# Start-up order of an adaptive-norm router kernel: condition weights, experts and the first transposes

## What is computed

```python
W = weights[condition]                       # one [128, 128] matrix of 16 for each sample
flat = einsum('bct,bcd->bdt', x, W).reshape(B * 128, 2048)
logits = flat @ router_weight.T + router_bias
topk_w, topk_idx = top_k(softmax(logits), 8)
w_dense = zeros(B * 128, 64).at[rows, topk_idx].add(topk_w)
out = x + (flat * topk_w.sum(-1) + w_dense @ expert_bias).reshape(x.shape)
```

## Time and profile before

| | |
|---|---|
| three runs | 558.46, 559.57 and 559.75 us, median 559.57 |
| the profiled execution's own time | 558.69 us |
| its span in the profile | 556.9 us |
| TensorE matmuls busy | 541.0 us, 97% of the span |
| VectorE, ScalarE, GpSimd busy | 471.2, 368.5 and 354.4 us |
| mean granted TensorE clock | 0.993 |

### The profile page before, as it was taken

The page is one execution under the profiler, slowest core; times in us unless marked ns, Lnnn a source line. Parts: engine busy times, 40 slices in busy tenths (PEclk is TensorE's granted clock), DMA queues, the critical chain, the costliest instruction groups (busy, mean ns, idle before and its releaser), DMA issues.

```text
span 556.9 us, 12892 instructions
## 1 busy us (share of the span) xinstructions
PE 541.0 (97%) x3360; PEld 477.0 (86%) x3360; DVE 471.2 (85%) x1055; ACT 368.5 (66%) x836; POOL 354.4 (64%) x326
## 2 busy tenths in 40 slices
PE   5879999999999999999999999999999999999997
PEld 5768888888888888888888888888888888888875
DVE  2488898988889988889988889898888998888975
ACT  3576666677666677666677666667666667766661
POOL 0176666766666776666776666676666677666676
PEclk9979999999999999999999999999999999999999
DMA  8986999888999888898888999888899888889245
GB/s 243 311 201 231 309 297 279 292 300 287 297 318 276 269 311 289 295 325 280 292 276 296 294 311 300 271 290 297 286 298 315 284 283 295 288 294 326 119 166 212
DMA packets 70850, 155.96 MB, mean 280 GB/s; under 512 B 6322, under 2 KB 45234, under 8 KB 62770
## 3 DMA queue, kind: packets, MB, share of 16 engines
q1 hardware_dynamic: 70834, 155.77, 85.6%
HBM read 88.64 MB, written 67.11 MB: 280 GB/s over the span
## 4 chain that ended last, share of the span: by engine, by line
PE 93%; DMA 3%; SPq 1%; ACT 1%; issue 1%; DVE 1%; ACTq 0%; DVEq 0%
PE zt_ps L337 21%; PE xt_ps L325 14%; PE p_ps L390 11%; PE p_ps L387 11%; PE p_ps L385 11%; PE p_ps L386 10%; PE p_ps L391 10%; PE scores_ps L360 2%; DMA out_sb<-L_ffn_expert_bias 2%; PE scores_ps L369 1%; PE scores_ps L351 1%; DMA cond_sb<-itok_B 1%; SPq L243 0%; SPq L244 0%; DVE xt_lo L546 0%
## 5 line engine op out<-in xcount | busy, mean ns | idle before, releaser
L681 POOL TENSOR_TENSOR x_lo<-x_sb,x_hi 128x512 fp32r<-128x512 f32 x256 | 327.0, 1308 | 176.2 <-ACT x_hi L459 176.2
L546 DVE TENSOR_TENSOR xt_lo<-xt_ps,xt_hi 128x512 fp32r<-128x512 f32 x256 | 175.7, 687 | 63.6 <-ACT xt_hi L451 60.8
L451 ACT CAST xt_hi<-xt_ps 128x512 fp32r<-128x512 f32 x256 | 148.2, 582 | 102.9 <-PE xt_ps L325 84.9
L612 DVE SCALAR_TENSOR_TENSOR out_sb<-p_ps,w_sum,x_sb 128x512 f32<-128x512 f32 x256 | 189.6, 740 | 6.2 <-PE p_ps L391 6.2
L459 ACT CAST x_hi<-x_sb 128x1024 fp32r<-128x1024 f32 x128 | 133.7, 1045 | 0.5 <-PE p_ps L391 0.5
L337 PE MATMUL zt_ps<-xt_hi,router_hl 128*128 128x256 f32 x512 | 129.6, 285 | 4.5 <-DVE xt_lo L546 4.5
L337 PE MATMUL zt_ps<-xt_lo,router_hl 128*128 128x256 f32 x512 | 129.2, 285 | 0.0
L325 PE MATMUL xt_ps<-ident,x_sb 128*128 128x128 f32 x784 | 119.2, 277 | 0.1
L385 PE MATMUL p_ps<-x_hi,w_hl 128*128 128x512 f32 x256 | 118.8, 464 | 0.0
L337 PEld LDWEIGHTS zt_ps<-xt_hi,router_hl 128*128 128x128 f32 x512 | 98.1, 192 | 11.0 <-DVE xt_lo L546 5.2
L337 PEld LDWEIGHTS zt_ps<-xt_lo,router_hl 128*128 128x128 f32 x512 | 98.4, 192 | 4.8
(11 more groups left out here) (38 smaller groups left out, 368.7 us busy)
## 6 DMA issues: line engine op xcount, KB each, us to landing
out<-out_sb SPq DMA_DIRECT2D x126, 512.0 KB, 4.2
x_sb<-x SPq DMA_DIRECT2D x62, 1024.0 KB, 6.8
x_turn<-x SPq DMA_DIRECT2D x120, 128.0 KB, 4.7
w_sb<-L_cond_weights SPq DMA_DIRECT2D x64, 64.0 KB, 5.3
x_sb<-x SPq DMA_DIRECT2D x4, 256.0 KB, 6.0
x_sb<-x SPq DMA_DIRECT2D x2, 512.0 KB, 8.0
out_sb<-L_ffn_expert_bias SPq DMA_DIRECT2D x2, 512.0 KB, 9.4
out<-out_sb SPq DMA_DIRECT2D x4, 256.0 KB, 2.5
```

The costliest lines, as they stand in the source:

```text
L451: act.copy(xt_hi[:, n % 2, :, r, :], xt_ps[v % 4][:, :].rearrange("p (q c) -> p q c", c=P)).then_inc(xt_hi_ready, 1)
L546: dve.tensor_tensor(xt_lo[:, n % 2, :, r, :], xt_ps[v % 4][:, :].rearrange("p (q c) -> p q c", c=P), xt_hi[:, n % 2, :, r, :].bitcast(F32) ...
L612: dve.scalar_tensor_tensor(out_sb[:, r, cols], p_ps[n % 2][:, :], w_sum[:, o % 2, r:r + 1], x_sb[:, (2 * o + r) % XRING, cols], ALU.mult, ...
L681: pool.tensor_tensor(x_lo[:, r, cols], x_sb[:, (2 * o + r) % XRING, cols], x_hi[:, r, cols].bitcast(F32), ALU.subtract).then_inc(x_lo_read ...
```

## The change

SP: the conditions are loaded third, ahead of the router's second half. The x pair of unit 1 is issued ahead of the wait for the conditions and of all weights; the weights of units 0 and 1 follow. TensorE: slot 0 of unit 0 is transposed right after the router's first half, and its cast and subtraction stand between the two halves of the router's cast and subtraction; the first route waits for the first half only, the third for both. Experts: the cast and subtraction leave ScalarE and VectorE; GpSimd makes four copies and four subtractions of 512 columns each, in the step of unit 1, between `w_low` of unit 1 and `x_low` of unit 0.

```diff
             load_first(0, slice(0, PIECE), first_loaded)
+            sp.dma_start(cond_sb[:, :], condition).then_inc(cond_loaded, 16)
             sp.dma_start(router_sb[:, HALF:T], router_weight[:, HALF:T]).then_inc(router_loaded[1], 16)
             load_first(1, slice(0, PIECE), first_loaded)
-            sp.dma_start(cond_sb[:, :], condition).then_inc(cond_loaded, 16)
             for r in range(2):
                 load_first(r, slice(PIECE, HALF), second_loaded)
             for r in range(2):
                 load_first(r, slice(HALF, T), x_loaded)
-            sp.wait_ge(cond_loaded, 16)
-            for r in range(2):
-                load_weights(0, 0, r)
             for r in range(2):
                 load(0, 1, r)
-            for r in range(2):
-                load_weights(0, 1, r)
+            sp.wait_ge(cond_loaded, 16)
+            for o in range(2):
+                for r in range(2):
+                    load_weights(0, o, r)
...
-            sp.wait_ge(router_in_ps, 1)
+            sp.wait_ge(router_in_ps, 2)
...
-            last.then_inc(router_in_ps, 1)
+                if q == TB // 2 - 1:
+                    last.then_inc(router_in_ps, 1)
+                if t == TB // 2 - 1:
+                    transposes(0, 0, 0)
...
-                    elif new:
+                    elif new and (i, v) != (0, 0):
                         transposes(m, i, v)
...
                         if i == 2 and v == 0:
-                            pe.wait_ge(expert_ready, 1)
+                            pe.wait_ge(expert_ready, PIECES)
                         project(m, i - 2, v)
...
-                        if i == 0 and v == 3:
-                            pe.wait_ge(router_ready, 2)
+                        if i == 0 and v in (3, 7):
+                            pe.wait_ge(router_ready, 1 + v // 7)
                         route(m, i, v // 2 - 1)
...
-            act.wait_ge(router_in_ps, 1)
             for g in range(2):
+                act.wait_ge(router_in_ps, g + 1)
                 act.copy(router_hl[:, g * TB // 2:(g + 1) * TB // 2, 0, :],
                          p_ps[g][:, :].rearrange("p (t e) -> p t e", e=E)).then_inc(router_hi_ready, 1)
+                if g == 0:
+                    xt_high(0, 0, 0)
...
-                    if i == 1 and v == 4:
-                        act.wait_ge(expert_loaded, 32)
-                        act.copy(expert_hl[:, :], expert_sb).then_inc(expert_hi_ready, 1)
...
                                   ALU.subtract).then_inc(router_ready, 1)
+                if g == 0:
+                    xt_low(0, 0, 0)
...
-                    if i == 1 and v == 6:
-                        dve.wait_ge(expert_hi_ready, 1)
-                        dve.tensor_tensor(expert_hl[E:2 * E, :], expert_sb[E:2 * E, :],
-                                          expert_hl[E:2 * E, :].bitcast(F32),
-                                          ALU.subtract).then_inc(expert_ready, 1)
...
+            def split_experts():
+                pool.wait_ge(expert_loaded, 32)
+                for n in range(PIECES):
+                    cols = slice(n * PIECE, (n + 1) * PIECE)
+                    pool.tensor_copy(expert_hl[:, cols], expert_sb[:, cols]).then_inc(expert_hi_ready, 1)
+                pool.wait_ge(expert_hi_ready, PIECES)
+                for n in range(PIECES):
+                    cols = slice(n * PIECE, (n + 1) * PIECE)
+                    pool.tensor_tensor(expert_hl[E:2 * E, cols], expert_sb[E:2 * E, cols],
+                                       expert_hl[E:2 * E, cols].bitcast(F32),
+                                       ALU.subtract).then_inc(expert_ready, 1)
+                pool.wait_ge(expert_ready, PIECES)
...
                     for r in range(2):
                         w_low(m, i, r)
+                if i == 1:
+                    split_experts()
                 if mid:
                     x_low(m, i - 1, 0)
```

More of the change, by code:

```diff
@@ L517, in step @@
                             w_high(m, i, r)
-                    if i == 1 and v == 4:
-                        act.wait_ge(expert_loaded, 32)
-                        act.copy(expert_hl[:, :], expert_sb).then_inc(expert_hi_ready, 1)
                     if mid and v == 1:
                         zt_copy(m, i - 1)
-                    if new:
+                    if new and (i, v) != (0, 0):
                         xt_high(m, i, v)
@@ L646, in step @@
                         if i == 2 and v == 0:
-                            dve.wait_ge(expert_ready, 1)
+                            dve.wait_ge(expert_ready, PIECES)
                         finish(m, i - 2, v)
```

## The result

The changed kernel takes 564.83 us (median; 564.53 to 565.16), the kernel before 559.66 on the same chips: ratio 1.0092, interval 1.0070 to 1.0115, so 5.2 us slower. 563.7 was forecast, in a range of 560.0 to 567.5. The profiled execution took 564.53 us and has a span of 562.7 us against 556.9, 5.8 more.

A forecast was written before the change was run, and what follows sets the result against it. TensorE, busy throughout 100 to 500 us, bounds the kernel, so early delays carry through one for one. First projection at 41.4 against 36.4 gives +5.0 us on the profiled 558.69: 563.7 us, range 560.0 to 567.5.

The forecast's parts named there:

- SP's order: SP's load queue: first weights land at 19.1, 5.6 us later; TensorE idles 6.3 us, second route at 20.9.
- Rival 1: Weight queue, 7 to 19 us: first weights do not wait for the second x pair; 557.2 us; chance 0.14.
- Conditions third, first slot between the halves: SP's loads and the first unit's slot 0: these moves cost nothing and gain nothing.
- The clock, first fall: TensorE after the 6.3 idle us: half clock from 20.9 to 27.2, for 6.26 us.
- Rival 2: TensorE's second route: the clock does not fall in the 6.3 idle us; +2.2 us, 560.9; chance 0.09.
- GpSimd as the last wait: Before the first projection: GpSimd's expert split ends at 40.1, the x subtraction the projection needs at 41.4.
- That is late next: GpSimd's expert copies and subtractions, 8.4 us, end at 40.1; the needed x subtraction takes 1.3 more, to 41.4.
- rival 3: TensorE idle from about 36.1 to 38.2 and 40.2 to 41.4: clock falls once more; 2.7 us, 566.4; chance 0.14.
- TensorE ready at 40.2: After the route at 38.2, a route and eight transposes end at 40.2; TensorE could project from there.
- The forecast 41.4: End of GpSimd's x subtraction that the first projection needs, compared with the mark of 36.4: +5.0 us.

The follow-up runs named there:

- e1: The changed kernel with the first unit's weights issued ahead of the second x pair again; median 557.95 us, ratio 0.9983.
- e2: The kernel before with only the second x pair issued ahead of the wait for the conditions and of all weights; median 565.26 us, ratio 1.0100.
- e4: The kernel before with only conditions third and the first unit's slot 0 between the router's halves; median 558.12 us, ratio 0.9971.
- e5: The changed kernel with GpSimd's four expert subtractions held until VectorE has made the first neg_max; median 566.50 us, ratio 1.0116.
- e9: The changed kernel with first weights ahead of the second x pair and only expert copies on GpSimd, VectorE subtracting; median 556.28 us, ratio 0.9934.
- e6: The changed kernel with 44 more identity transposes ahead of TensorE's second route; median 563.37 us, ratio 1.0069.
- e8: The kernel before with 26 more identity transposes ahead of the second unit's route that starts at 31.32; median 559.15 us, ratio 0.9998.
- e3: The kernel before with only the experts' split moved to GpSimd, SP's order as before; median 559.39 us, ratio 0.9987.
- e11: The kernel of e9 with VectorE's expert subtraction in two halves of 1024 columns, the first ahead of slot 5; median 557.63 us, ratio 0.9963.
- e12: The kernel of e9 with the first weights issued ahead of the last pieces of the first x pair; median 557.48 us, ratio 0.9958.

## Why the prediction was right, and where not

**SP's order: right in place and size.** The wait moved to 19.16 (forecast 19.1), TensorE's idle stretch is 6.21 us (6.3), the restart at 21.13 (20.9). e1 and e2 show that this part is all of the loss. The landings of the earlier trace rows were enough to see it (the issue of the last x piece began at 4.85, not 5.1, so it landed at 13.3, just ahead of the weights, not with them). Rival 1, that the weights would not wait for the second x pair, fell: the loads of x and of the weights of the first 17 us landed in the order of their issue in every profile. Not all loads did: in the kernel before, a piece of x that a DMA turns, issued at 18.71, landed after 12.7 us, at 31.4, ahead of weights issued at 18.33 (14.6 us, 32.9). So the order that the prediction read from its rows holds for these loads, not for the queue as a whole. The Trainium skill, "DMA: Bandwidth & Descriptors", section "Queues, rings and completion order", cited with that rival, says that completion is not first in, first out; the trace agrees for the turned pieces (31.4 ahead of 32.9), not for x and weights.

**Conditions third, first slot between the halves: costed at nothing**, and e4's profile agrees (557.0 against 556.9); the third slot again waits for its DMA, at 10.13 in the changed kernel. The 0.29% of e4's runs are the part that this leaves unexplained.

**The clock, first fall: mis-sized.** Taken as 6.26 us of half clock from the restart on, as in the kernel before. TensorE worked at half clock only from 21.13 to about 24.4 (0.4 us of half clock make the 0.90 of 24 to 26). The clock had fallen at about 17.6, in the idle stretch (0.89 from 16 to 18), and what passed of it there cost nothing. The split of the second unit's weights therefore ended at 30.48, 1.2 us earlier than forecast. Rival 2, no fall, fell itself.

**GpSimd as the last wait: wrong in this kernel.** "That is late next" is the step that failed. A copy took 0.615 us against the 0.70 taken (the bounds were 0.52 and 1.31), the four subtractions 4.97 against 5.24; with the earlier start the split ended at 37.77, not 40.1, and the first x subtraction at about 39.4. The projection did not wait for it: it began at 41.53, when TensorE had done its route, transposes and kept weights from 37.88 on. In e1 and e5, where TensorE was ready sooner or GpSimd was held, the first projection did wait for its x subtraction: the mechanism exists, its term was too long for this kernel. The estimate of 0.44 us for the loop of a copy, worked out in the prediction from the Trainium skill, "GPSIMD Engine Reference", section "Elementwise — side-by-side cycle accounting", leaves 0.17 of the measured 0.615 for the dispatch; no run separates the two.

**What stood in its place.** TensorE itself, and two things that the sum did not hold. VectorE's `neg_max` was held for 0.85 us by GpSimd's subtraction. And the clock fell again behind 2.99 idle us, which was rival 3, at a chance of 0.14; it cost (1.95 - 0.94) + (1.71 - 1.03) = 1.7 us, not the 2.7 of that rival, as the products of the projection already ran at full clock. The prediction had TensorE ready at 40.2; with 1.2 less from the first fall, 0.85 and 1.7 more that is 41.5, and 41.53 was measured. The forecast 41.4 was GpSimd's. That the two times agree is luck: GpSimd's x subtraction was ready 2.0 us sooner than forecast, and TensorE 1.3 us later.

A third, smaller wait makes the rest. TensorE stood before the fourth of the five products until 42.70, for the low part of the kept weights, so the first projection lasted 1.91 us (41.53 to 43.44) instead of 1.15. With it +5.0 forecast became +5.8 in the span; at the medians it is +5.2. The cause and the sign are right on the evidence of e1 and e2; the size is right in part because errors cancel.

## What to carry to other kernels

Before a load is moved ahead in a queue that is backed up, ask what it is moved ahead of: a 64 KB load that something waits for, put behind 2 MB, landed 5.6 us later although it was issued 0.5 us earlier. When work goes to GpSimd, look at what stands behind it in GpSimd's own order (the x subtraction that the first projection waited for in e1) and at which VectorE instructions run beside it (`neg_max` in the changed kernel): here the copies alone gave a gain (e9), and the subtractions with them took it back (e1). A half clock in a profile is worth its price only if TensorE is what the next step waits for: 2.0 us in the profile of e6, at most 0.7 of 2.7 in that of e8.

## What the runs showed of the hardware

Two short VectorE instructions stood still while GpSimd ran a two-input subtraction: `neg_max` 1.02 us instead of 0.17, `e_kept` up to 1.33 instead of 0.22. The shorter one-input copies held `neg_max` too, but less: 0.42 us in e1, 0.45 in e3, 0.25 in e9, 0.19 in e11. VectorE's subtractions that read PSUM stayed at 0.69 beside the same GpSimd work. The Trainium skill, "GPSIMD Engine Reference", section "Specifications", says that GpSimd shares its SBUF interfaces with VectorE and contends with VectorE instructions that have two SBUF inputs or run in a 2-port mode. `e_kept` has two SBUF inputs, so the trace agrees; that `neg_max`, with one, runs in such a mode is not shown here.

It goes the other way as well, already in the kernel before:

```profile
31.57 12.13 POOL L681 TENSOR_TENSOR x_lo<-x_sb,x_hi 128x512 fp32r<-128x512 f32 x8 [8.25 <-ACT x_hi L459]
...
32.73 2.29 DVE L636 TENSOR_TENSOR expert_hl<-out_sb,expert_hl 64x2048 fp32r<-64x2048 f32 x1
```

VectorE's expert subtraction, with two inputs in SBUF, takes 2.29 us (its halves in e11, with GpSimd idle, 1.22 each), and of GpSimd's eight x subtractions, which take 10.04 us together in e1, the one that starts at 32.81, just behind it, takes 3.35 us instead of 1.3. In e2, e8, e9 and e12 it takes 3.35 or 3.36. In all these pairs the instruction that had started first went on, and the other stood.

Whether the clock falls is not told by the idle time alone: after 2.99 us it was at 0.51 (changed kernel), after 3.00 us at 1.00 (e6); after 2.39 us at 0.50 (e1), after 2.43 us at 1.00 (e3).
